# An attention and quantised feed-forward kernel on one core: the bias store moved to GpSimd's queue, three weight loads and sums taken early, and two lists of the tail reordered

## The reference

```python
# attention: C = 128 channels, T = 256 positions, 16 heads of 8
Q, K, V = (proj(Wq), proj(Wk), proj(Wv))
att = einsum('bhqd,bhkd->bhqk', Q, K) / sqrt(Dh) + b[0]
att = att * m + (1.0 - m) * NEG_INF          # m: the mask over keys
y = einsum('bhqk,bhkd->bhqd', softmax(att), V)
# feed-forward: H = 256, I = 1024
def activation_quant(x): s = 127 / clip(max(abs(x), axis=-1), EPS); return clip(round(x * s), -128, 127) / s
def weight_quant(w):     s = 1.0 / clip(mean(abs(w)), EPS);         return clip(round(w * s), -1, 1) / s
h = silu(bit_linear(x, w_gate)) * bit_linear(x, w_up)
h = rms_norm(h, ln_weight)
return x_in + bit_linear(h, w_down)
```

## Time and profile before

| | us |
|---|---|
| median of 3 runs | 163.2 |
| the profiled execution's own time | 163.05 |
| its span | 161.2 |
| TensorE matmul busy (1402 instructions) | 143.8 (89%) |
| VectorE busy (204) | 136.7 (85%) |
| ScalarE busy (255) | 125.4 (78%) |
| GpSimd busy (185) | 104.0 (65%) |
| granted TensorE clock | 1.0 throughout |

### The profile page before, as it was taken

The page is one execution under the profiler, slowest core; times in us unless marked ns, Lnnn a source line. Parts: engine busy times, 40 slices in busy tenths (PEclk is TensorE's granted clock), DMA queues, the critical chain, the costliest instruction groups (busy, mean ns, idle before and its releaser), DMA issues.

```text
span 161.2 us, 4126 instructions
## 1 busy us (share of the span) xinstructions
PE 143.8 (89%) x1402; PEld 66.7 (41%) x1402; DVE 136.7 (85%) x204; ACT 125.4 (78%) x255; POOL 104.0 (65%) x185
## 2 busy tenths in 40 slices
PE   6968998998999999999997999979889966999893
PEld 2644553433333333433333333332323342665672
DVE  6788998898999989789997999993398788999972
ACT  3042377899899899989889889886999966998970
POOL 5889625848818818806898997822313579689920
PEclk9999999999999999999999999999999999999999
DMA  3994896457255345533233000000000000001012
GB/s 107 278 206 97 262 294 191 141 141 213 71 135 147 85 108 173 192 76 82 62 74 86 3 3 4 5 5 4 3 0 4 0 0 2 0 33 39 33 65 98
DMA packets 19904, 14.19 MB, mean 88 GB/s; under 512 B 2360, under 2 KB 18800, under 8 KB 19884
## 3 DMA queue, kind: packets, MB, share of 16 engines
q1 hardware_dynamic: 16940, 11.52, 25.7%
q10 hardware_dynamic: 2624, 2.17, 5.2%
q0 software_dynamic: 320, 0.25, 1.0%
HBM read 6.17 MB, written 1.07 MB: 45 GB/s over the span
## 4 chain that ended last, share of the span: by engine, by line
PE 55%; DVE 12%; ACT 11%; POOL 8%; issue 7%; DMA 4%; SPq 1%; ACTq 0%; DVEq 0%; POOLq 0%
PE y_ps L1073 14%; PE s_ps L1034 13%; ACT probs L570 5%; PE t_ps L1053 5%; DVE maxes L944 4%; PE s_ps L1164 4%; PE t_ps L1006 3%; DMA bias_scr<-bias_parts 2%; PE t_ps L1094 2%; ACT hid_sq L675 2%; PE y_ps L1114 2%; PE t_ps L1183 2%; PE t_ps L1015 2%; DVE hid L878 2%; PE t_ps L1203 2%
## 5 line engine op out<-in xcount | busy, mean ns | idle before, releaser
L944 DVE TENSOR_REDUCE maxes<-s_ps 128x4 f32<-128x1024 f32 x64 | 76.0, 1218 | 6.8 <-PE s_ps L1034 6.6
L570 ACT ACTIVATE probs<-t_ps 128x512 f32<-128x512 f32 x118 | 65.9, 591 | 8.6 <-PE t_ps L1053 6.2
L1034 PE MATMUL s_ps<-k_st,q_st 64*128 64x256 bf16 x256 | 44.7, 274 | 1.0 <-DMA k_st<-bias_scr 0.5
L1053 PE MATMUL t_ps<-q_st,k_st 64*128 64x256 bf16 x236 | 42.5, 274 | 3.3 <-ACT probs L570 1.6
L1073 PE MATMUL y_ps<-probs,v_pad 128*18 128x256 f32 x512 | 38.6, 384 | 0.2 <-ACT probs L570 0.2
L1034 PEld LDWEIGHTS s_ps<-k_st,q_st 64*128 64x128 bf16 x256 | 15.8, 94 | 29.6 <-issue 16.0
L1164 PE MATMUL s_ps<-w_q,ffn_x 128*128 128x512 bf16 x64 | 17.2, 380 | 2.9 <-DVE hid L878 2.4
L523 POOL TENSOR_TENSOR hw<-hid,ln_bc 128x512 f32<-128x512 f32 x8 | 10.2, 1273 | 12.0 <-DVE hid L867 8.9
L1053 PEld LDWEIGHTS t_ps<-q_st,k_st 64*128 64x128 bf16 x236 | 14.0, 94 | 8.3 <-ACT probs L570 3.6
L438 POOL TENSOR_SCALAR nm_parts<-maxes 128x16 bf16<-128x16 f32 x16 | 3.3, 207 | 21.6 <-DVE maxes L944 21.5
L1073 PEld LDWEIGHTS y_ps<-probs,v_pad 128*18 128x18 f32 x512 | 9.6, 96 | 14.2 <-issue 11.6
(11 more groups left out here) (116 smaller groups left out, 245.6 us busy)
## 6 DMA issues: line engine op xcount, KB each, us to landing
q_st<-parts SPq DMA_DIRECT2D x48, 64.0 KB, 2.7
k_st<-parts SPq DMA_DIRECT2D x33, 64.0 KB, 2.4
w_f<-in_wgT ACTq DMA_DIRECT2D x2, 512.0 KB, 4.7
w_f<-in_wuT SPq DMA_DIRECT2D x2, 512.0 KB, 4.3
w_f<-in_wdT SPq DMA_DIRECT2D x2, 512.0 KB, 4.9
out<-o_sb SPq DMA_DIRECT2D x8, 128.0 KB, 1.7
k_st<-parts ACTq DMA_DIRECT2D x15, 64.0 KB, 3.1
x_sb<-in_x SPq DMA_DIRECT2D x2, 256.0 KB, 3.9
```

What stands on the lines that cost most here:

```text
L570: act.activation(probs[:, t % NP_RING].rearrange("p e t -> p (e t)"), src, ACT.Exp, scale=SCALE)\
L944: dve.tensor_reduce(dst[:, :, s, :], s_ps[:, c % 2], AX.X, ALU.max).then_inc(s_maxed, 1)
L1034: mm = pe.matmul(s_ps[:, c % 2, i, e, :], q_st[b % RING][rows, hp, qt * P:qt * P + P], k_st[b % RING][rows, hp, :], start=True, stop=True)
L1053: mm = pe.matmul(t_bank(bank["t", t])[:, e * T:e * T + T], k_st[b % RING][rows, hp, kt * P:kt * P + P], q_st[b % RING][rows, hp, :], start ...
```

## The change

- The bias store (`bias_scr`) is issued by GpSimd and no longer by SP. GpSimd's two `affine_select` of the identity matrices stand before the bias computation and no longer behind it.
- x3 moves on SP from before the first high part to behind `load_bias(0)` and w0. w0 and w1 move from ScalarE's queue to SP's; w0 stands behind `load_bias(0)`, w1 and w2 before mask 2. Loads w3 to w5 stand in steps -1 to 1.
- The weight sums move to (-1, 4), (-1, 6), (-1, 7), (0, 6), (1, 6), (2, 3), the total to (2, 5), the scales to (2, 7).
- GpSimd's nine weight operations spread over steps 3 to 7.
- The fourth stack is cleared by GpSimd in step -1 and no longer by VectorE in the prologue.
- Four idle matmuls of 128x512 before the steps are left out.
- In the tail VectorE's `normalize_y(7)` moves behind unit 5's product, and `hidden_steps(1)`, `hidden_maximum(2)` and `hidden_steps(2)` move one product later each. ScalarE takes the first transposed hidden block before the square of batch 3.

```diff
-WEIGHT_SUM_SLOTS = {(-1, 5): 0, (-1, 7): 1, (0, 6): 2, (1, 6): 3, (2, 6): 4, (3, 3): 5}
-WEIGHT_TOTAL_SLOT = (3, 5)
+WEIGHT_SUM_SLOTS = {(-1, 4): 0, (-1, 6): 1, (-1, 7): 2, (0, 6): 3, (1, 6): 4, (2, 3): 5}
+WEIGHT_TOTAL_SLOT = (2, 5)
...
         def load_high(queue, b, side):
...
+            elif b == RING - 1:
+                queue.wait_ge(last_zeroed, 2)
...
             load_x(2)
-            load_x(3)
             load_high(sp, 0, 0)
-            sp.wait_ge(bias_step, 7)
-            sp.dma_start(bias_scr, bias_parts[:, :, :, :].to_broadcast([B, 2, 3, T])).then_inc(bias_stored, 16)
             load_low(sp, 0, (0,))
             load_bias(0)
+            load_weights(sp, 0)
+            load_x(3)
             load_rows(1)
             load_bias(1)
             load_high(sp, 1, 0)
             load_low(sp, 1, (0,))
+            load_weights(sp, 1)
+            load_weights(sp, 2)
             load_mask(sp, 2)
...
-                if n < 3:
-                    load_weights(sp, n + 3)
+                if n < 2:
+                    load_weights(sp, n + 4)
...
+            pool.wait_ge(ident_ready, 2)
+            for m in (ident_b, ident_f):
+                pool.affine_select(...)
             pool.wait_ge(mask_in, 32)
...
-            pool.wait_ge(ident_ready, 2)
-            for m in (ident_b, ident_f):
-                pool.affine_select(...)
+            pool.wait_ge(bias_step, 7)
+            pool.dma_start(bias_scr, bias_parts[:, :, :, :].to_broadcast([B, 2, 3, T])).then_inc(bias_stored, 16)
...
-            weight_steps = {4: ((), (0, 1)), 5: ((2, 3), (4, 5)), 6: ((6, 7), (8,))}
+            weight_steps = {3: ((), (0,)), 4: ((1,), (2,)), 5: ((3,), (4,)), 6: ((5,), (6,)), 7: ((7, 8), ())}
...
+                if n == -1:
+                    pool.memset(q_st[RING - 1][:, :, :].rearrange("p h t -> p (h t)").bitcast(f32), 0.0).then_inc(last_zeroed, 1)
+                    pool.memset(k_st[RING - 1][:, :, :].rearrange("p h t -> p (h t)").bitcast(f32), BF16_ONES)\
+                        .then_inc(last_zeroed, 1)
...
-            for q in range(2):
-                load_weights(act, q)
             act.wait_ge(k_zeroed, 3)
...
             for b in range(AHEAD, B):
+                if b == AHEAD:
+                    take_hidden_t(0)
                 if b < B - 1:
                     square_hidden(b)
                     hidden_mean(b)
-                if b == AHEAD:
-                    take_hidden_t(0)
...
-            for r in range(1, RING):
+            for r in range(1, RING - 1):
                 clear_stacks(r)
...
-                    if (n, k) == (3, 7):
+                    if (n, k) == (2, 7):
                         mean_weights()
...
-                        if u == 4:
+                        if u == 5:
                             normalize_y(B - 1)
-                        if u == 5:
                             weight_high_half(2)
-                            hidden_steps(1)
...
-            hidden_maximum(AHEAD - 1)
             for b in range(AHEAD, B):
                 gate_times_up(2 * b)
-                hidden_steps(b - 1)
+                if b == AHEAD:
+                    hidden_steps(1)
+                    hidden_maximum(AHEAD - 1)
+                else:
+                    hidden_steps(b - 1)
                 gate_times_up(2 * b + 1)
                 weight_high_half(b)
                 if b == AHEAD:
+                    hidden_steps(AHEAD - 1)
                     scale_y(B - 1)
                     scale_late_tokens()
...
             project_qk(3)
-            keep_array_busy(4)
```

More of the change, by code:

```diff
@@ L213, in adaln_ffn_kernel @@
         k_zeroed = sem("k_zeroed")
+        last_zeroed = sem("last_zeroed")
         v_zeroed = sem("v_zeroed")
@@ L404, in _ @@
             pool.memset(ident_f[:, :], 0.0).then_inc(ident_ready, 1)
+            pool.wait_ge(ident_ready, 2)
+            for m in (ident_b, ident_f):
+                pool.affine_select(out=m[:, :], in_=m[:, :], compare_op=ALU.not_equal, fill=1.0,
+                                   base=0, pattern=[[-1, P]], channel_multiplier=1).then_inc(ident_ready, 1)
             pool.wait_ge(mask_in, 32)
@@ L420, in _ @@
                 .then_inc(bias_step, 1)
-            pool.wait_ge(ident_ready, 2)
-            for m in (ident_b, ident_f):
-                pool.affine_select(out=m[:, :], in_=m[:, :], compare_op=ALU.not_equal, fill=1.0,
-                                   base=0, pattern=[[-1, P]], channel_multiplier=1).then_inc(ident_ready, 1)
+            pool.wait_ge(bias_step, 7)
+            pool.dma_start(bias_scr, bias_parts[:, :, :, :].to_broadcast([B, 2, 3, T])).then_inc(bias_stored, 16)
             pool.memset(ones_f[:, :], 1.0).then_inc(small_const, 1)
@@ L487, in load_constant_rows @@
                 if b < RING:
-                    pool.wait_ge(q_zeroed, b + 1)
-                    pool.wait_ge(k_zeroed, b + 1)
+                    pool.wait_ge(last_zeroed, 2)
                     pool.dma_start(q_st[b % RING][BIAS_ROWS], ones6[:, :, :].to_broadcast([6, NHP, T]))\
```

## The result

The changed kernel takes 167.13 us in the median of four runs (166.33 to 167.96) against 163.43 (162.35 to 165.45) for the kernel before, run beside it: 1.0251 times, 95% interval 1.0208 to 1.0294. (The ratio is not the quotient of the two medians: a run in a slower state, the 165.45 of the kernel before, is left out of it.) It is slower, and my range ended at 164.3.

The account below looks back on a forecast made before the run. The prediction saw no single bound: TensorE, VectorE and ScalarE run close together in a fixed order. From 163.05 us it summed +0.2 (start), -0.6 (sums), +0.6 (GpSimd's weight operations), -0.75 (tail) to 162.5 us, range 160.9 to 164.3.

Parts of the forecast that it names:

- The start: Up to the first exponential: an earlier bias doesn't carry, as SP's issues hold the maximum rows; 0.2 us slower.
- the granted clock is 1.0 in every window; nothing: Prologue: leaving out the four idle matmuls costs nothing, as TensorE's 0.5 us bias wait stood behind them at full clock.
- what stays idle in between is TensorE and VectorE: Before the first exponential: the wait for the maximum rows idles these engines, not ScalarE; first exponential about 27.0 against 26.8.
- The first rival: Start gained in full: first exponential 1.0 us earlier, 161.3 us in all; chance 0.20.
- Steps 2 and 3: Moving the sums and total leaves step 3 without any: 25.20 us become 24.65, a gain in round numbers of 0.6.
- GpSimd's weight operations: Steps 4 and 5: a new wait costs 1.2 us, a removed one gives 0.6; net 0.6 slower.
- so 0.5 was made up by the buffers; I take 1.7 - 0.5 = 1.2: Step 4, slot (4, 6): TensorE's new 1.7 us wait costs only 1.2, buffers absorbing 0.5.
- the last rival: Step 4's new wait is absorbed by ScalarE's 1.6 us of slack: 161.9 us in all; chance 0.09.
- The tail: After the last maxima: reordered lists remove most of VectorE's three waits; 0.75 us faster.
- 1.0 us that nobody was waiting for: Tail: ScalarE's copies move into its wait of 2.61 us; 1.0 us of them held nobody up.
- The third rival: Tail: GpSimd, with 0.2 us of room, takes the gain of 0.75; 163.2 us in all; chance 0.12.
- The late bias store: Prologue rival: the store on GpSimd's queue lands late, first exponential 1.7 us late; 164.6 us in all; chance 0.12.

Follow-up runs that it names:

- x3_busy: The changed kernel with eleven idle matmuls where TensorE would wait for the first maximum rows: 1.0161 times the kernel before.
- x2_loads_act: The changed kernel with the first three weight loads (w0, w1, w2) issued by ScalarE's queue, not SP's: 1.0286 times the kernel before.
- w2_late_total: The kernel before with GpSimd's weight operations spread, the sixth sum at (3, 6), the total at (4, 3), the scales at (4, 5): 1.0005 times the kernel before.
- r1_three_undone: The changed kernel with eleven idle matmuls, ScalarE's old tail list and no weight operation between step 4's split and maxima: 1.0001 times the kernel before.
- x1_ops: The changed kernel with GpSimd's weight operation 1 moved from step 4's start to the end of step 3: 1.0192 times the kernel before.
- t1: The kernel before with both tail lists (VectorE's and ScalarE's) of the changed kernel: 0.9991 times the kernel before.
- t2: The kernel before with ScalarE's tail list of the changed kernel, VectorE's as before: 0.9988 times the kernel before.
- t3: The kernel before with VectorE's tail list of the changed kernel, ScalarE's as before: 0.999 times the kernel before.
- d2_w1_act: The changed kernel's start with w2 behind the rows, w1 on ScalarE's queue, weight operations spread, late total, old tail lists: 0.9998 times the kernel before.

## Why the prediction was wrong

*The start, +0.2 forecast, +1.75 measured.* The bias landed early, SP's list ended on time, x3 and the memsets cost nothing: these steps held. Of the miss of 1.55, 0.45 is the first exponential, which came 0.65 later and not 0.2: the rows landed 2.27 us after their issue, where I had taken 1.94 from a stretch with fewer transfers. The other 1.10 is a term that I had put at nothing. The sentences that failed are "the granted clock is 1.0 in every window; nothing", said of the idle matmuls, and "what stays idle in between is TensorE and VectorE", which priced the hole only by when it ends. It was 2.79 us long, and the clock was halved. x3_busy shows the 1.10 by giving it back. That the clock was 1.0 everywhere was a reading of one execution of a kernel whose waits were 1.23 us long at most; it said nothing of one with 2.8, nor even of that kernel's other runs, of which one in four has a fall. The first rival (start gained in full) fails at the same place. In x2_loads_act SP's list was 2.6 us shorter, and the transfers, with the rows' own readiness, held the rows back all the same.

*Steps 2 and 3, -0.6: right.* w2_late_total shows the reason to be right as well.

*GpSimd's weight operations, +0.6 forecast, +1.4 measured.* The wait was where I had put it, 1.87 us against 1.7. The mis-sized term is "so 0.5 was made up by the buffers; I take 1.7 - 0.5 = 1.2". I had one case, a wait of 0.86, which I counted as 1.1, that cost 0.59, and took the difference for an allowance. The new wait cost 2.0 us, more than its own length, and r1_three_undone gives 1.93 of it back; in x1_ops a wait of 0.88 cost 1.06. x1_ops shows that an operation of 1.9 us has no free place near a `negate_maxes` in step 3's end either: the last rival (wait absorbed) had ScalarE's slack for it, which was not the engine that mattered.

*The tail, -0.75 forecast, +0.8 measured.* VectorE did run ahead, by 0.54 us. "1.0 us that nobody was waiting for" was true of ScalarE's copies and false of what they release: they keep TensorE's transposes in a place that is otherwise empty. t1, t2 and t3 show that it takes both lists for the hole (1.97 us against 0.98 and 0.51), and the hole and the fall behind it are worth 0.6 of the tail (53.42 against 52.83). The gain itself went before that: VectorE's two-column product now met GpSimd's rounding and took 0.76 us longer. The third rival, GpSimd taking the gain, named the engine and very nearly the price, 0.75, by luck: its mechanism was GpSimd's list, and what the trace shows is two operations that don't run side by side. It had no term for the clock.

*The late bias store* did not happen. The Trainium skill (SBUF — State Buffer, section SBUF: two separate sides) speaks of DMAs from GpSimd's queue that can't be written while VectorE runs an operation in a two-port mode; it names copies, casts and `tensor_scalar` for that, and says that `tensor_tensor` did not stall a DMA. Here the store landed 2.6 us after its issue, beside a subtraction (`tensor_tensor`) and a memset of VectorE. So the trace agrees with the section, and it was the prediction that stretched its rule to these operations. The same section says that the pair is an exclusive lock, and that the one that starts first keeps it for a whole instruction. The trace agrees where the starts are well apart: the product that began 0.16 us behind the rounding took 0.99 instead of 0.23, the one 0.35 behind took 1.30 instead of 0.69. With starts 0.04 to 0.09 us apart the one recorded as first was the stretched one in some traces (the rounding, 1.64 instead of 1.12, in the kernel before; the limit, 0.84 instead of 0.34, in the changed one) and not in w2_late_total, so there the recorded order doesn't tell who came first.

What stays open: whether a filler in the tail's hole would hold the clock there was not tried. Why the waits of 1.87 and 0.88 us in step 4 cost 0.15 to 0.2 us more than their length, and the one of 0.86 in step 5 of the kernel before a third less, isn't settled, nor why a hole of 1.87 us in step 4 left the clock at 1.00 where one of 1.96 in the tail, and in d2_w1_act waits of 0.69 and 1.49, did not. The median of the changed kernel lies 0.8 above its profiled execution, and two of its runs have a third fall; in which hole, I can't say, as they have no trace.

## What to carry to other kernels

A wait on an engine that is nearly full is priced by what stands behind it, at its whole length until a row shows slack on that same engine, and where TensorE is the one that waits, by its clock too: without a row that shows a hole of the new length at full clock, a fall is a case with a price, not nothing. Idle matmuls and work off the path may be what keeps a hole short; before removing or moving them, see what TensorE has left to do in that place. Where two engines share a port, a list shifted by a few tenths of a microsecond can be worth half a percent with no instruction changed. So a gain or loss of that size in one profile is not yet the edit's: look at the same place in several traces, and at the whole kernel's time over many runs.

## What was not expected of the hardware

- Around holes of 3.52, 3.08, 2.79, 2.63, 2.59 and 1.96 us on TensorE, and in one execution of 1.49 us with one of 0.69 ahead of it, the granted clock fell to 1.2 GHz, for 3.4 us or twice that. The fall began between 0.7 us ahead of the hole's end (2.63) and 1.25 us behind it (2.79). A hole of 1.87 in step 4 left it at 2.4 GHz, as did waits of 1.23 us and less in the profiled execution of the kernel before. With idle matmuls in the first hole it stayed up. In step 0 one fall of 3.4 us cost 0.75 to 1.10 us, one of 6.8 us 1.8 to 1.9.
- A product over two columns took 0.99 us on VectorE instead of 0.23 while GpSimd was in an operation of 1.12 us over 1024; the two ended within 0.03 us of each other (138.84 and 138.81), in all nine traces with that list alike.
- A load of the maximum rows was used 4.6 us after its issue with the DMA engines busy for 1.0 to 1.1 of every stretch of 2 us, and 1.94 after it where they had room (share 0.37 from 24 to 26 us in the kernel before).
